# Four rotating buffers for the straight and turned rows of a decoder layer's projections, and the first stack loads sent in small pieces

## The reference

```python
x = x + attn(layernorm(x), w_qkv, w_out)            # 16 heads of 32, causal               ("first")
x = x + xattn(layernorm(x), ctx, pos, ...)          # 32 heads of 16, keys from ctx, axial rotation ("cross")
x = x + ffn(layernorm(x), ...)                      # rms, 16 heads of 32, rotation, causal ("rotary"), then mixture of experts

def rotate(q, cos, sin):                            # what the change touches, for q and for k
    return q * cos + swap(q) * sin                  # swap: pairs (cross) or halves of a head (rotary), with signs
```

## Time and profile before

| what | value |
|---|---|
| median of three executions | 2207.22 us |
| profiled execution | 2207.37 us |
| its span | 2205.6 us, granted TensorE clock 0.958 |
| PE busy | 2028.7 us (92%) |
| DVE busy | 1222.6 us (55%) |
| ACT busy | 907.4 us (41%) |
| POOL busy | 708.4 us (32%) |
| ring of projections, cross | about 450 to 582 us of the span |
| ring of projections, rotary | about 1038 to 1192 us of the span |

### The profile page before, as it was taken

How to read it: one execution, slowest core, us unless ns; L and a number is a source line. 1 busy time by engine, 2 the same in 40 slices (tenths; PEclk the granted TensorE clock), 3 DMA queues, 4 the chain that set the end, 5 groups by cost and what they waited for, 6 DMA issues and landing times. The chain is left out here.

```text
span 2205.6 us, 31497 instructions
## 1 busy us (share of the span) xinstructions
PE 2028.7 (92%) x10679; PEld 1359.8 (62%) x10679; DVE 1222.6 (55%) x2649; ACT 907.4 (41%) x1699; POOL 708.4 (32%) x610
## 2 busy tenths in 40 slices
PE   7999999788599999996997999979999999999998
PEld 6876666566333334334776666657888788555664
DVE  6446666377789798875876666544323153221221
ACT  3435544355377676773443544434212221111111
POOL 0004655257423132322564755601000000223332
PEclk9997999989699999998997999989999999999999
DMA  5557776356654545444457766452011045233331
GB/s 196 176 200 160 167 157 134 112 181 247 231 139 117 141 109 154 102 126 124 175 193 224 169 151 153 117 221 97 33 63 56 21 179 215 61 66 61 61 62 37
DMA packets 150706, 297.15 MB, mean 135 GB/s; under 512 B 24530, under 2 KB 43092, under 8 KB 149524
## 3 DMA queue, kind: packets, MB, share of 16 engines
q1 hardware_dynamic: 112676, 241.64, 37.3%
q10 hardware_dynamic: 29136, 34.87, 5.9%
q0 software_dynamic: 8736, 18.62, 4.5%
HBM read 181.55 MB, written 102.50 MB: 129 GB/s over the span
## 5 line engine op out<-in xcount | busy, mean ns | idle before, releaser
L1259 ACT ACTIVATE cross_c_prob<-bank 128x512 f32<-128x512 f32 x512 | 271.1, 598 | 118.5 <-PE bank L1098 117.5
L1300 DVE TENSOR_REDUCE row_max<-bank 128x2 f32<-128x1024 f32 x256 | 299.9, 1212 | 28.1 <-PE bank L1067 27.0
L1686 PE MATMUL bank<-moe_hT,moe_w 128*128 128x512 f32 x1056 | 252.3, 395 | 9.1 <-DVE moe_w L1933 4.6
L1067 PE MATMUL bank<-stack 48*128 48x512 f32 (+4 forms) x768 | 210.1, 455 | 44.3 <-PEq L70 28.7
L1098 PE MATMUL bank<-stack 56*128 56x512 f32 (+4 forms) x768 | 234.0, 430 | 12.9 <-DMA stack<-rotary_c_max_rows 4.1
L1686 PEld LDWEIGHTS bank<-moe_hT,moe_w 128*128 128x128 f32 x1056 | 200.3, 191 | 52.5 <-issue 5.0
L1098 PEld LDWEIGHTS bank<-stack 56*128 56x128 f32 (+1 forms) x768 | 118.6, 193 | 145.3 <-ACT cross_c_prob L1259 71.1
L1774 PE MATMUL bank<-moe_w_e,moe_hT_e 128*128 x624 | 194.4, 465 | 4.4 <-DMA moe_w_e<-in_experts_packed 3.8
L1067 PEld LDWEIGHTS bank<-stack 48*128 48x128 f32 (+1 forms) x768 | 104.2, 202 | 125.4 <-DVE row_max L1300 49.6
L1774 PEld LDWEIGHTS bank<-moe_w_e,moe_hT_e 128*128 128x128 f32 x624 | 116.2, 191 | 66.2 <-issue 8.2
L1296 DVE CUSTOM_DVE_ANT_0 first_c_masked<-bank,later 128x128 f32<-128x128 f32 (+3 forms) x256 | 115.4, 485 | 72.0 <-PE bank L1067 71.0
(11 more groups left out here) (361 smaller groups left out, 4034.1 us busy)
## 6 DMA issues: line engine op xcount, KB each, us to landing
moe_w_e<-in_experts_packed SPq DMA_DIRECT2D x8, 2176.0 KB, 8.8
qk_parts<-first_p_parts SPq DMA_DIRECT2D x32, 512.0 KB, 2.7
stack<-qk_parts SPq DMA_DIRECT2D x64, 256.0 KB, 6.8
qk_parts<-cross_p_parts SPq DMA_DIRECT2D x32, 512.0 KB, 2.7
stack<-qk_parts SPq DMA_DIRECT2D x256, 64.0 KB, 2.5
qk_parts<-rotary_p_parts SPq DMA_DIRECT2D x32, 512.0 KB, 2.7
moe_raw<-in_shared_packed SPq DMA_DIRECT2D x11, 768.0 KB, 11.5
stack<-qk_parts SPq DMA_DIRECT2D x16, 512.0 KB, 5.2
```

Source lines behind the costliest of these rows:

```text
L1067: last = nc.tensor.matmul(bank[:, 0 : width_q(m)], q_stack[slot][r : r + PRODUCT_ROWS, at, m * P : (m + 1) * P], k_stack[slot][r : r + PRO ...
L1259: nc.scalar.activation(probability(g, step // HEADS_AT_ONCE, step % HEADS_AT_ONCE), psum[bank_at["score", n]][:, 0 : S - q0], ACT.Exp).the ...
L1300: nc.vector.tensor_reduce(row_max[:, g % 2, m, j - 1 : j + 1], c.banks[:, first : first + WIDE, :], AX_X, ALU.max).then_inc(s.max_done, 1)
L1686: last = nc.tensor.matmul(psum[bank][:], weights(pa, f, k), hT[p % 2][:, pb, k, :], start=m == 0, stop=m == len(steps) - 1)
```

## The change

In cross and rotary `straight` gets four buffers instead of two, and `turned` gets four, which lie in the room of `raw0`. `swapped` and `parts` keep two. ACT's straight(i) and POOL's cos(i) wait for what happened four steps earlier, and before the first cos POOL waits until the third weight matrix is split. The order of instructions on ACT, DVE, POOL and PE stays. On SP, from step n = 10 on, two DMAs (cross) or one DMA (first, rotary) of a stack are issued ahead of each store of q or k, until the first three (two) stacks are through.

```diff
+SENDS_OF_STACK = 5
-def load_stack(sp, a, batch, g):
+def load_stack(sp, a, batch, g, wanted=None):
+    sent = itertools.count()
     def send(stack, half, first, last, src, every=1):
+        n = next(sent)
+        if wanted is not None and n not in wanted:
+            return
...
-            straight, swapped, turned = sb("straight", [P, 2, S]), sb("swapped", [P, 2, S]), sb("turned", [P, 2, S])
+            ROPE_SLOTS = 4
+            straight, swapped = sb("straight", [P, ROPE_SLOTS, S]), sb("swapped", [P, 2, S])
+            turned = a.raw0[:].rearrange("p (a n) -> p a n", n=S)
...
-        STACK_AT = {at: g for g, at in enumerate(((BODY - 2, 1), (BODY - 2, 3), (BODY - 1, 1))[: t.early_stacks])}
+        SENDS, SENDS_AT_ONCE, FIRST_SEND_AT = SENDS_OF_STACK * t.halves, t.halves, 10
...
-                            if what == "q" and (bi, m) in STACK_AT:
+                            n = bi * n_qk + 2 * m + (what == "k")
+                            at = (n - FIRST_SEND_AT) * SENDS_AT_ONCE
+                            if at == 0:
                                 for st in qk_stored:
                                     sp.wait_ge(st, 16 * (qk_before + n_qk // 2))
-                                load_stack(sp, a, loop * BODY, STACK_AT[bi, m])
+                            if 0 <= at < SENDS * t.early_stacks:
+                                load_stack(sp, a, loop * BODY, at // SENDS, range(at % SENDS, at % SENDS + SENDS_AT_ONCE))
...
-                            if i >= 2:
-                                act.wait_ge(s.swap_made, i - 1)
-                                act.wait_ge(s.cos_made, i - 1)
+                            if i >= ROPE_SLOTS:
+                                act.wait_ge(s.swap_made, i - ROPE_SLOTS + 1)
+                                act.wait_ge(s.cos_made, i - ROPE_SLOTS + 1)
...
                             pool.wait_ge(s.straight_made, i + 1)
-                            if i >= 2:
-                                pool.wait_ge(s.parts_lo, i - 1)
-                            nc.gpsimd.tensor_tensor(turned[:, i % 2], straight[:, i % 2], cos_t[:, i // n_qk if cross else 0], ALU.mult).then_inc(s.cos_made, 1)
+                            if i == 0:
+                                pool.wait_ge(s.lo_made, 3)
+                            if i >= ROPE_SLOTS:
+                                pool.wait_ge(s.parts_lo, i - ROPE_SLOTS + 1)
+                            nc.gpsimd.tensor_tensor(turned[:, i % ROPE_SLOTS], straight[:, i % ROPE_SLOTS], cos_t[:, i // n_qk if cross else 0], ALU.mult).then_inc(s.cos_made, 1)
```

More of the change, by code:

```diff
@@ L8 @@
 from contextlib import ExitStack
+import itertools
 import numpy as np
@@ L381, in _ @@
                                 load_context(bi + 2)
-                            if what == "q" and (bi, m) in STACK_AT:
+                            n = bi * n_qk + 2 * m + (what == "k")
+                            at = (n - FIRST_SEND_AT) * SENDS_AT_ONCE
+                            if at == 0:
                                 for st in qk_stored:
                                     sp.wait_ge(st, 16 * (qk_before + n_qk // 2))
-                                load_stack(sp, a, loop * BODY, STACK_AT[bi, m])
-                            n = bi * n_qk + 2 * m + (what == "k")
+                            if 0 <= at < SENDS * t.early_stacks:
+                                load_stack(sp, a, loop * BODY, at // SENDS, range(at % SENDS, at % SENDS + SENDS_AT_ONCE))
                             sp.wait_ge(s.parts_hi, n + 1)
@@ L491, in high @@
                             act.wait_ge(qk_stored[n % 2], 16 * (qk_before + n // 2))
-                        nc.scalar.activation(parts[:, n % 2, 0], turned[:, n % 2], ACT.Copy).then_inc(s.parts_hi, 1)
+                        nc.scalar.activation(parts[:, n % 2, 0], turned[:, n % ROPE_SLOTS], ACT.Copy).then_inc(s.parts_hi, 1)
                     def trig(bi):
@@ L567, in _ @@
                         if rope:
-                            if i >= 2:
-                                act.wait_ge(s.swap_made, i - 1)
-                                act.wait_ge(s.cos_made, i - 1)
+                            if i >= ROPE_SLOTS:
+                                act.wait_ge(s.swap_made, i - ROPE_SLOTS + 1)
+                                act.wait_ge(s.cos_made, i - ROPE_SLOTS + 1)
                             if rotary:
                                 bias = bias_q[:, m : m + 1] if what == "q" else bias_raw[:, 1, m : m + 1]
-                                nc.scalar.activation(straight[:, i % 2], bank[:], ACT.Identity, bias=bias, scale=scale).then_inc(s.straight_made, 1)
+                                nc.scalar.activation(straight[:, i % ROPE_SLOTS], bank[:], ACT.Identity, bias=bias, scale=scale).then_inc(s.straight_made, 1)
                             else:
-                                nc.scalar.activation(straight[:, i % 2], bank[:], ACT.Copy, scale=scale).then_inc(s.straight_made, 1)
+                                nc.scalar.activation(straight[:, i % ROPE_SLOTS], bank[:], ACT.Copy, scale=scale).then_inc(s.straight_made, 1)
                             if i >= 2:
@@ L718, in rotate @@
                         dve.wait_ge(s.sin_made, i + 1)
-                        nc.vector.tensor_tensor(turned[:, i % 2], turned[:, i % 2], swapped[:, i % 2], ALU.add).then_inc(s.rotated, 1)
+                        nc.vector.tensor_tensor(turned[:, i % ROPE_SLOTS], turned[:, i % ROPE_SLOTS], swapped[:, i % 2], ALU.add).then_inc(s.rotated, 1)
                     def low(i):
                         dve.wait_ge(s.parts_hi, i + 1)
-                        nc.vector.tensor_tensor(parts[:, i % 2, 1], turned[:, i % 2], parts[:, i % 2, 0].bitcast(F32), ALU.subtract).then_inc(s.parts_lo, 1)
+                        nc.vector.tensor_tensor(parts[:, i % 2, 1], turned[:, i % ROPE_SLOTS], parts[:, i % 2, 0].bitcast(F32), ALU.subtract).then_inc(s.parts_lo, 1)
                     def weights_low(n):
@@ L770, in _ @@
                             swap = [r ^ 1 for r in range(32)] if cross else [(r + 16) % 32 for r in range(32)]
-                            nc.vector.stream_shuffle(swapped[:, i % 2], straight[:, i % 2], swap).then_inc(s.swap_made, 1)
+                            nc.vector.stream_shuffle(swapped[:, i % 2], straight[:, i % ROPE_SLOTS], swap).then_inc(s.swap_made, 1)
                             if i >= 2:
```

## The result

The changed kernel takes 2229.97 us in the median (2228.51 to 2235.58, four runs), the kernel before 2208.47 in its four (2203.44 to 2210.84). The ratio is 1.0105, with a 95% interval from 1.0079 to 1.0131: slower, by 21.5 us. The forecast was 2223 with a range from 2201 to 2233. The profiled execution took 2228.51 us (span 2226.7, granted clock 0.953), and its span is 21.1 us longer than that of before.

A forecast was written before the change was run, and what follows sets the result against it. PE leads, stalled inside batches by DVE's lateness and in last batches by the chain POOL, DVE, ACT. 13.1 + 9.2 - 3.4 - 3.3 = +15.6 on the profiled 2207.37 gave 2223 us, range 2201 to 2233.

The forecast's parts named there:

- Turns of DVE and POOL: Batches 0 to 2: the engines alternate, so sin(i) goes ahead of rotate(i-1), costing DVE 1.1 us more every step.
- the stepping: Cross batch 1, step by step from shuffle(8): the context's `hT_lo` ends at 504.0 instead of 500.76, taken as +3.25 us.
- The six middle batches: Batches 0 to 2 of cross and rotary: DVE's added waits cost +13.1 and +9.2 us, +22.3 in all.
- Rival B: DVE keeps its turn, POOL gets it only in a real pause of DVE: +2.5 us, 2210; chance 0.18.
- Rival C: Added DVE waits fall into its pauses, middle cross batches save 0.6 each, tails shorten: -8.5 us, 2199; chance 0.17.
- Pieces at no cost: Stack loads on SP: pieces are issued while SP would wait for low(n), so 0 us (bounds -1 to +3).
- The wait for the third split: Start of rotary: the split (L728) ends at 1043.94, before the first straight is finished, so 0 us.
- Four buffers, the last batch: Last cross and rotary batches: 3.4 us per step, stores' waits included, so -3.4 and -3.3 us.
- The clock term that I left out: PE after its longer pauses: what they cost in clock, left out of the sum with no size given.
- rival D: PE's longer pauses drop its clock, next products 1 to 2 us slower in each of six batches: 2232; chance 0.08.
- the 1.1 us of the forecast: Rotary: rotate(19) stands before the reciprocal that ACT needs for the rows PE then transposes: +1.1 us.

The follow-up runs named there:

- the first experiment: The changed kernel with two buffers for straight and turned instead of four, stack loads still in pieces: 2209.68 us, ratio 0.9994 to the kernel before.

## Why the prediction was right, and where its sizes were off

**Turns of DVE and POOL: right.** Rotate went to 1730 ns in cross and 1708 in rotary (predicted 1.7), low to 882 and 922 (I had it fall to 0.8; it rose from 864 and 831). The stretch from shuffle(8) to `hT_lo` took 17.68 us; the stepping had given 17.7. PE's wait ahead of the transposes in batch 1 grew to 6.65 (6.7), that for v in rotary to 4.80 (4.9). The six middle batches together cost +23.9 where I had +22.3. The Trainium skill, "SBUF — State Buffer", section "Who interferes with whom", says that issue order decides who blocks; the moved rotate agrees: with the same four buffers and the same instructions, rotate's mean is 1730 or 1224 ns, by its place in the order alone.

**Rival B** (DVE keeps its turn) falls with rotate's mean. **Rival C** (the last batches decide) falls too: rotate didn't stay under 0.9 us, and the last batches gave back 0.4 us together, not 6.7. **Pieces at no cost**: right, by the first experiment. **The wait for the third split** costs nothing either: the split ends at 1047.15 (L741, 1044.86 + 2.29), PE's first product of rotary starts at 1051.18.

**The step that failed is "Four buffers, the last batch".** Its rhythm was right: cos comes every 3.4 us. The timeline of the last cross batch:

```profile
565.14 0.76 DVE L784 STREAM_SHUFFLE cross_p_swapped<-cross_p_straight 128x512 f32<-128x512 f32 x1
...
571.54 1.74 POOL L829 TENSOR_TENSOR raw<-cross_p_straight,axial_cos 128x512 f32<-128x512 f32 x1
...
574.94 1.75 POOL L829 TENSOR_TENSOR raw<-cross_p_straight,axial_cos 128x512 f32<-128x512 f32 x1
...
593.72 0.69 DVE L732 TENSOR_TENSOR raw<-raw,cross_p_swapped 128x512 f32<-128x512 f32 x1
595.10 0.69 DVE L737 TENSOR_TENSOR cross_p_parts<-raw,cross_p_parts 128x512 fp32r<-128x512 f32 x1 [0.70 <-ACT cross_p_parts L505]
```

Two things came on top. The chain's end is longer: from the start of cos(31) (588.49) to the end of low(31) (595.79) it takes 7.3 us, not 5.5, mostly since rotate(31) stands behind low(30) in DVE's order, and that one waits for high(30). The chain from shuffle(24) is therefore 30.65 us instead of the 29.4 that I took (578.2 - 548.83; before, 32.74). And the batch starts later: shuffle(24) comes 6.14 us after PE's first product (565.14 - 559.00), where it came 3.69 after it (548.83 - 545.14). This is +2.45, and with the other and 0.3 us to the core it turns -3.4 into +0.7. In rotary PE ends on time, 32.9 us after its first product, but v3 and low(31) take 4.3 more and not 2.2: a held rotate (1.76 at 1208.18) ends 0.95 us after PE does, and v2, low(30) and rotate(31) still stand in front of them.

**The clock term that I left out** is that +2.45. PE's products from 559.57 start 0.42 us apart (559.99 - 559.57), those from 545.14 of before 0.23 to 0.24. The granted clock behind the first product of a batch shows the same. Two stretches of the kernel before come first (starts of cross batch 1 and of the last one), then three of the changed kernel (batches 1, 2 and the last); the column before the last two is the granted clock:

```profile
481.30:484.30 3.00, 3.00 (x7) 2.42 (x8) 2.15 (x3) 0.00 (x0) 2.31 (x2) 0.51 0.26 105
545.20:548.20 3.00, 3.00 (x13) 2.46 (x14) 2.14 (x3) 0.01 (x1) 2.31 (x2) 1.00 0.26 102
...
484.30:487.30 3.00, 3.00 (x13) 2.49 (x14) 2.76 (x3) 0.00 (x0) 1.63 (x1) 1.00 0.36 145
521.10:524.10 3.00, 3.00 (x7) 2.44 (x8) 2.74 (x3) 0.00 (x0) 1.63 (x1) 0.50 0.35 141
559.00:562.00 3.00, 3.00 (x7) 2.42 (x8) 2.76 (x3) 0.00 (x0) 1.63 (x1) 0.50 0.35 142
```

The term has both signs, and the near hit of the middle batches hides that. In batch 1 the kernel before had the slow start: its shuffle(8) came 5.03 us after PE's first product (486.31 - 481.28), now 3.68 (487.96 - 484.28), which gives back 1.35. The end of that batch, from `hT_lo` to PE's next first product, grew by 2.3 us (513.86 - 500.76 = 13.10 before, 521.08 - 505.64 = 15.44 now) where I had stepped to 1.65. So +4.2 against my +4.9 is a stepped middle that was right, an end 0.7 too small and a start that I didn't count; that the total came so close is in part luck. In batch 2 it is the other way: shuffle(16) comes 5.12 us after the first product (526.20 - 521.08), 3.68 before (517.54 - 513.86), +1.44 of the 1.7 by which the batch exceeds the forecast. Batch 0 starts slowly in both kernels. Together the starts cost +2.5 (-1.35 + 1.44 + 2.45); with them the sum would have been about 2225.5, not rival D's 2232.

In rotary the slow products came too: behind the waits of 4.80 and 4.93 us for v, ten or more products ran 0.43 us apart (granted clock 0.50 from 1120.70 to 1124.90, against 1.00 from 1102.90 to 1105.70 before; in batch 2 the kernel before had eight of them too). They cost little, since the rows that PE transposes next were themselves late by the 1.1 us of the forecast: ACT starts them 3.42 us behind PE's first product after that wait (1123.53 - 1120.11), 2.36 before (1105.21 - 1102.85). In batch 1 PE's transposes start 1.66 us behind ACT's start on these rows (1125.19 - 1123.53) where it was 0.85 (1106.06 - 1105.21), so the clock cost at most 0.8 us there.

That a slow start follows from the 2.9 us pause alone isn't shown: 484.28 has a pause as long and products of 0.39 right behind it. Nor did I find the cause of the 2.4 us by which all else is shorter; 0.8 of it lies ahead of the cross ring, 1.2 between the two rings and 0.3 behind them.

## What to carry to other kernels

A buffer for an engine that isn't the bottleneck is no free gift: it changes when its instructions stand ready, and where two engines exclude each other it decides which of them pays. Ahead of a deeper ring, look in the timeline for which short operation on the critical engine will find a long one of the other already waiting; if there is one, reorder the critical engine first (here -0.33% with cos bound to low(i - 2) as before, where the buffers brought +1.05%). And an end of phase that looks like a throughput limit has a tail in program order: step it to the last instruction.

## What the runs showed of the hardware beyond that

A DVE operation on little data is held too: the shift, 128 x 4 elements from two operands in SBUF, took 1.02 us beside a product (500.54), while the reciprocal ahead of it took 0.17. Operations with an operand in PSUM weren't held where this could be seen: the four `hT_lo` of the changed kernel at 1087.69 took 2.71 us, 0.68 each, while a cos ran its 1.29 at 1087.84 beside them. A GpSimd product over an eighth of the columns still had a mean of 713 ns, turns included, against 1672 for the full one, so shortening the operation buys less than its share. And on PE of the changed kernel, of three pauses of 2.89 to 2.91 us in front of a cross batch, two were followed by products 0.42 us apart (granted clock 0.50, so 1.2 GHz) and one by products 0.23 apart (granted clock 1.00, so 2.4 GHz).
